# Rotary attention layer of a four-layer kernel: the rotation's work divided anew over ScalarE, GpSimd and VectorE

## The chip, the cores and the metric

The kernel runs on one core of one Trainium2 chip. The metric is the device time of one execution in microseconds, lower is better; each version is executed several times and the median counts.

## The reference

Four layers work on `x`, two batches of 256 tokens with 512 features. Each layer adds a gated attention and then a gated feed-forward part. The attentions differ; the second one (L1) rotates its queries and keys:

```
def _rope(x):                       # x: (B, H, S, 128)
    ...
    cos = concatenate([cos(ang), cos(ang)], axis=-1)
    sin = concatenate([sin(ang), sin(ang)], axis=-1)
    x1, x2 = (x[..., :64], x[..., 64:])
    rot = concatenate([-x2, x1], axis=-1)
    return x * cos + rot * sin

queries = _rope((q @ Wq.T) per head)    # 32 heads of 128
keys    = _rope((k @ Wk.T) per head)    # 8 key heads of 128, each for 4 query heads
scores  = queries . keys * 128 ** -0.5, causal (256 x 256, of 512 context rows only the first 256 count)
ctx     = softmax(scores) @ values
x       = x + tanh(g_xattn[1]) * (ctx @ Wd.T)
```

## The kernel before

One program, written engine by engine: each of the four attentions is a `Layer`, and `attn_sync`, `attn_tensor`, `attn_vector`, `attn_scalar` and `attn_gpsimd` write the queue of one engine each. Engines run their queues in order; they meet only through counted semaphores (`Counter`), one per kind of product: `q_mm` for a finished query projection, `q_f` for a rotated query before its sum, `q_sum` for the sum, `s_norm` for normalised probabilities, `wq_lo` for the low part of a piece of Wq, and so on.

All matrix products are done in three parts to keep precision: each operand is split in a high part (written by ScalarE's `activation`) and a low part (source less high part). The low parts of weights (`wq_lo`, `wkv_lo`, `wo_lo`) are GpSimd's, those of data (`q_lo`, `k_lo`, `v_lo`, `o_lo`, `pT_lo`) VectorE's. TensorE multiplies high by high, high by low and low by high.

The work goes by groups: a group is one key head with its four query heads. `walk` writes a prologue for group 0, then a hardware loop over pairs of groups, then the last two groups. A head has four slots, `j` = 0 to 3 (batch x half of the tokens), and the engines are shifted against each other: in slot `j` of a head the scores of two slots ahead are begun, and the probabilities of this slot are transposed and used. In the rotary layer:

- slot 1 of head h: TensorE projects the query of two heads ahead into the one bank `psQ`; it needs `wq_lo` and the bank free (`q_f`).
- the end of the same slot: VectorE rotates out of `psQ` into `qscr` (`q_front`, L739 to L741): feature d lies on partition d, so the exchange of halves is a product whose output lies 64 partitions away from its input. Three instructions: times cosine (128 partitions), upper and lower half times sine (64 each).
- slot 2: GpSimd first normalises the probabilities of slot 0 of the next head (L1041), then adds the two products (`q_sum`, L1058), and in heads 1 and 2 makes a low part of Wo (L1054).
- slot 3: ScalarE makes the query's high part (L949), which waits for `q_sum`. GpSimd normalises the next probabilities and makes a low part of Wq (L1048), for which the projection of the next head waits.
- slot 0 of the next head: VectorE makes the query's low part (L789).
- the next group's key is projected in slot 3 of head 1 and rotated in the same way (`use`, kind "k": VectorE into `scr`, sum on GpSimd L1066, high part on ScalarE L984, low part on VectorE L800); the values follow in head 2 (L839) and, transposed, in head 3 (ScalarE L996, VectorE L842).
- head 0, slots 1 to 3: TensorE's output projections of the group before (12 matmuls each), which wait for the output's low part (L794).

TensorE's matmuls are all written by a helper (L333), its transposes by L635. Cosines and sines lie in `mask_sb` behind the causal mask.

Of the kernel before, what the change touches and what calls it, by code (L numbers as in the profile page):

```python
# [24 lines left out]
ALU = mybir.AluOpType  # L25
ACT = mybir.ActivationFunctionType
AX = mybir.AxisListType

P = 128
B = 2  # L30
SQ = 256
# [45 lines left out]
            "av_mm o_hi o_lo x_mm x_act x_free k_f k_hi k_lo k_r k_diag").split()  # L77
# [44 lines left out]
class Layer:  # L122


    def __init__(self, index, sems):
# [18 lines left out]
        n = self.n  # L144
# [11 lines left out]
                     k_r=2 * n if self.rms else 0, k_diag=2 * n if self.rms else 0)  # L156
# [5 lines left out]
         self.x_free, self.k_f, self.k_hi, self.k_lo, self.k_r, self.k_diag) = counters  # L162
# [71 lines left out]
def program(nc, a, out, scratch):  # L234

    ctx = ExitStack()
    with ctx:
# [495 lines left out]
        def rotated(dve, src, dst):  # L733

            h = P // 2
            src = src.rearrange("p (b m) -> p b m", b=B)
            cos, sin = (trig[:, i, :].unsqueeze(1).broadcast_to([P, B, SQ]) for i in (0, 1))
            by_cos, by_sin = (dst[:, i, :].rearrange("p (b m) -> p b m", b=B) for i in (0, 1))
            dve.tensor_tensor(by_cos, src, cos, ALU.mult)  # L739
            dve.tensor_tensor(by_sin[0:h], src[h:P], sin[h:P], ALU.mult)  # L740
            return dve.tensor_tensor(by_sin[h:P], src[0:h], sin[0:h], ALU.mult)  # L741

        def attn_vector(dve, L):
# [32 lines left out]
            def q_front(g, h):  # L776
                L.q_mm.wait(dve, g.at(4, h + 1))
                L.q_f.inc(rotated(dve, psQ[:, :], qscr))
# [23 lines left out]
            def use(g, what, gp):  # L802
# [7 lines left out]
                if kind == "t" or (kind == "k" and not L.masked):  # L810
                    L.x_act.wait(dve, L.count(g, act_letters, what))
                elif kind == "k" and L.rms:
                    L.k_f.wait(dve, L.count(g, "k", what))
                else:
                    L.x_mm.wait(dve, k + 1)
# [9 lines left out]
                elif kind == "k" and L.rope:  # L825
                    ins = rotated(dve, X, scr)
# [89 lines left out]
        def attn_scalar(act, L):  # L916
# [27 lines left out]

            def q_high(g, h):
# [23 lines left out]
            def use(g, what, gp):  # L969
# [5 lines left out]
                if kind == "k" and L.rms:  # L975
                    L.x_mm.wait(act, k + 1)
                    L.k_f.inc(act.activation(ksq[:, i, :], X, ACT.Square))
                elif (kind == "k" and L.rope) or kind == "b":
# [20 lines left out]
            def prologue():  # L999
                for kind, piece in (("wq", 0), ("wkv", 0), ("wkv", 1), ("wq", 1)):  # L1000
                    w_high(kind, Group(0), piece)
                L.vec_dma.wait(act, L.n_vec)
                q_high(Group(0), 0)
                w_high("wq", Group(0), 2)
                for u in L.first:
                    use(None, u, Group(0))
                q_high(Group(0), 1)
                for j in range(L.ahead):
                    row_exp(Group(0), 0, j)

            def head(g, h):
                for j in range(4):
# [10 lines left out]
                    for u in L.slot_uses(g, h, j):  # L1023
                        if u[0] == "b" or (u[0] == "k" and L.rope):
                            late.append((g, u, g.to(1)))
                        elif u[0] not in ("out", "q"):
                            use(g, u, g.to(1))
# [4 lines left out]
                    if j == L.q_slot and L.step(g, h, 0, 8) and not L.rope:  # L1032
                        q_high(*L.step(g, h, 0, 8)[:2])
# [4 lines left out]
        def attn_gpsimd(pool, L):  # L1038
# [17 lines left out]
            def q_sum(g, h):  # L1056
                L.q_f.wait(pool, g.at(4, h + 1))
                L.q_sum.inc(pool.tensor_tensor(qscr[:, 0, :], qscr[:, 0, :], qscr[:, 1, :], ALU.add))  # L1058

            def use(g, what):  # L1060
# [553 lines left out]
```

How the kernel before makes its waits and increments, by code:

```python
    def wait(self, eng, value):  # L112
        if isinstance(value, int) and value <= 0:
            return
        eng.wait_ge(self.sem, value + self.base)
# [205 lines left out]
        def after(dve, ins):  # L322
            own[0] += 1
            ins.then_inc(dve_self, 1)
            dve.wait_ge(dve_self, own[0])
# [11 lines left out]
        def start_sync(sp):  # L338
            sp.dma_start(ident[:, :], a["c_ident"]).then_inc(const_dma, 16)
            sp.dma_start(ones[:, :], a["c_ones"]).then_inc(const_dma, 16)
            sp.dma_start(x_sb[:, :, :], a["x"].rearrange("b (t p) d -> p (b t) d", p=P)).then_inc(const_dma, 16)
            sp.dma_start(gates[:, 0:4], a["g_xattn"].partition_broadcast(P)).then_inc(gate_dma, 16)
            sp.dma_start(gates[:, 4:8], a["g_ffn"].partition_broadcast(P)).then_inc(gate_dma, 16)
            for c in range(DC):
                if c >= 2:
                    sp.wait_ge(ctx_lo, c - 1)
                sp.dma_start(p_sb[:, (c % 2) * 1024:(c % 2 + 1) * 1024],
                             a["ctxT"][:, c, :]).then_inc(ctx_dma[c % 2], 16)
# [1 line left out]
        def start_vector(dve):  # L350
            dve.memset(half[:, :], -0.5).then_inc(half_done, 1)
            for c in range(DC):
                dve.wait_ge(ctx_dma[c % 2], 16 * (c // 2 + 1))
                f = p_sb[:, (c % 2) * 1024:(c % 2 + 1) * 1024]
                dve.tensor_copy(cT_hi[:, c, :], f).then_inc(ctx_hi, 1)
                dve.wait_ge(ctx_hi, c + 1)
# [785 lines left out]
        def f0_tensor(pe):  # L1142
            pe.wait_ge(f0_w, 1)
            for t in range(NT):
```

## Time and profile before

| | |
|---|---|
| median of 3 executions | 2450.9 us (2448.56 to 2453.86) |
| the profiled execution | 2446.57 us, its span 2444.7 us |
| mean granted TensorE clock | 0.932 |
| busy in the span | PE 2058.0, DVE 1512.9, ACT 1034.7, POOL 1030.0 us |
| the rotary attention layer | about 715 to 1204 us |

PE is TensorE, PEld its weight loads, DVE VectorE, ACT ScalarE, POOL GpSimd, SP the engine that issues transfers. The span is the time from the first to the last instruction. A row with "idle before" gives how long the engine stood still just ahead of an instruction and which instruction of another engine ended that; "issue" means that the profile shows none. `L739` is line 739 of the kernel. The trace is of one execution, the median of others.

### The profile page before, as it was taken

To read this page: it belongs to the slowest core of one execution; us is meant where nothing else is said; L and a number is where in the kernel's file an instruction comes from. 1 tells how busy PE (TensorE), PEld (TensorE's weight loads), DVE (VectorE), ACT (ScalarE), POOL (GpSimd) and SP (SyncE) were. 2 spreads that over 40 slices of the span, in tenths; PEclk is the share of its full clock that TensorE was granted. 3 is DMA by queue.
4 is the path that set the end of the run, shared out by engine and by line. 5 is a ranking of instruction groups with operands and counts; after the bars stand their busy time and mean duration, and the time that the engine had idled before them with its cause. 6 is when DMAs were issued, how large, how long until landed. Compare 5 with 4: busy or idle time off the path is not lost.

```text
span 2444.7 us, 33604 instructions
## 1 busy us (share of the span) xinstructions
PE 2058.0 (84%) x10874; PEld 1700.0 (70%) x10874; DVE 1512.9 (62%) x2993; ACT 1034.7 (42%) x2320; POOL 1030.0 (42%) x955
## 2 busy tenths in 40 slices
PE   4898888988547878788888899997689999999986
PEld 3777777776435666666665788886567787787874
DVE  4777777777667666666533455554547766676664
ACT  2655565555314333333312344443135544455440
POOL 2555455554325444444332343333135544455540
PEclk9999999999868888888898999998789999999998
DMA  3212222121111111110021010000111100111001
GB/s 123 66 40 66 78 65 65 45 72 49 52 65 44 44 44 43 43 44 31 11 80 54 4 32 28 11 17 1 49 52 40 44 28 25 41 40 44 28 4 40
DMA packets 47042, 106.95 MB, mean 44 GB/s; under 512 B 6016, under 2 KB 21888, under 8 KB 43056
## 3 DMA queue, kind: packets, MB, share of 16 engines
q1 hardware_dynamic: 46896, 105.14, 13.6%
q8 instruction: 75, 1.23, 0.2%
q14 instruction: 71, 0.58, 0.1%
HBM read 98.37 MB, written 6.75 MB: 43 GB/s over the span
## 4 chain that ended last, share of the span: by engine, by line
PE 47%; issue 18%; DVE 14%; POOL 10%; ACT 7%; DMA 2%; SPq 0%; POOLq 0%; ACTq 0%; DVEq 0%
PE psX L333 18%; PE psS L333 7%; PE psQ L333 7%; PE psO L333 7%; POOL p_sb L1041 4%; PE psT L635 4%; DVE pT_lo L773 2%; ACT pT_hi L943 2%; POOL wo_lo L1054 2%; ACT dq_space L408 2%; POOL qscr L1058 1%; PE psT L333 1%; DVE nmax L763 1%; POOL wq_lo L1048 1%; ACT p_sb L936 1%
## 5 line engine op out<-in xcount | busy, mean ns | idle before, releaser
L1041 POOL TENSOR_TENSOR p_sb<-p_sb,rrec 128x512 f32<-128x512 f32 (+2 forms) x448 | 445.3, 994 | 950.5 <-DVE rrec L769 948.9
L943 ACT ACTIVATE pT_hi<-psT 128x512 fp32r<-128x512 f32 (+2 forms) x448 | 245.0, 547 | 413.7 <-PE psT L635 412.7
L773 DVE TENSOR_TENSOR pT_lo<-psT,pT_hi 128x512 fp32r<-128x512 f32 (+2 forms) x448 | 280.8, 627 | 113.2 <-ACT pT_hi L943 113.2
L333 PE MATMUL psO<-pT_hi,v_hi 128*128 128x256 f32 (+1 forms) x832 | 260.0, 313 | 61.4 <-DVE pT_lo L773 31.6
L635 PE MATMUL psT<-ident,p_sb 128*128 128x128 f32 x1600 | 262.0, 283 | 44.5 <-POOL p_sb L1041 44.3
L936 ACT ACTIVATE p_sb<-p_sb,nbias 128x512 f32<-128x512 f32 (+2 forms) x256 | 150.8, 589 | 270.9 <-DVE nbias L761 270.6
L635 PEld LDWEIGHTS psT<-ident,p_sb 128*128 128x128 f32 x1600 | 199.1, 144 | 94.1 <-POOL p_sb L1041 59.1
L333 PE MATMUL psX<-wo_hi,oT_hi 128*128 128x512 f32 (+1 forms) x448 | 187.0, 417 | 65.5 <-issue 65.5
L333 PE MATMUL psO<-pT_hi,v_lo 128*128 128x256 f32 (+1 forms) x832 | 239.7, 288 | 1.1 <-issue 1.1
L333 PE MATMUL psO<-pT_lo,v_hi 128*128 128x256 f32 (+1 forms) x832 | 240.1, 289 | 0.0
L333 PE MATMUL psQ<-xnT_hi,wq_hi 128*128 128x512 f32 (+1 forms) x448 | 198.8, 444 | 42.6 <-POOL wq_lo L1048 42.6
L333 PEld LDWEIGHTS psO<-pT_hi,v_hi 128*128 128x128 f32 (+1 forms) x832 | 157.5, 189 | 80.5 <-DVE pT_lo L773 65.4
L333 PE MATMUL psS<-kT_hi,q_hi 128*128 128x512 f32 (+2 forms) x448 | 178.9, 399 | 36.4 <-ACT p_sb L936 27.0
L936 ACT ACTIVATE p_sb<-psS,nbias 128x512 f32<-128x512 f32 (+1 forms) x192 | 145.3, 757 | 149.3 <-DVE nbias L765 149.3
L333 PE MATMUL psQ<-xnT_hi,wq_lo 128*128 128x512 f32 (+1 forms) x448 | 188.1, 420 | 0.0
L333 PE MATMUL psQ<-xnT_lo,wq_hi 128*128 128x512 f32 (+1 forms) x448 | 187.3, 418 | 0.0
L333 PE MATMUL psX<-wo_hi,oT_lo 128*128 128x512 f32 (+1 forms) x448 | 181.7, 406 | 0.0
L333 PE MATMUL psX<-wo_lo,oT_hi 128*128 128x512 f32 (+1 forms) x448 | 181.4, 405 | 0.0
L819 DVE SCALAR_TENSOR_TENSOR x_sb<-psX,gates,x_sb 128x512 f32<-128x512 f32 x112 | 83.9, 749 | 144.8 <-PE psX L333 144.8
L1048 POOL TENSOR_TENSOR wq_lo<-wq_f,wq_hi 128x512 fp32r<-128x512 f32 (+1 forms) x112 | 150.8, 1347 | 37.1 <-ACT wq_hi L925 37.1
L1054 POOL TENSOR_TENSOR wo_lo<-wo_f,wo_hi 128x512 fp32r<-128x512 f32 (+1 forms) x112 | 146.4, 1307 | 43.7 <-ACT wo_hi L931 43.1
L333 PE MATMUL psS<-kT_hi,q_lo 128*128 128x512 f32 (+2 forms) x448 | 164.7, 368 | 0.0
(313 smaller groups left out, 4845.8 us busy)
## 6 DMA issues: line engine op xcount, KB each, us to landing
wq_f<-in_a_wq SPq DMA_DIRECT2D x96, 256.0 KB, 2.6
wo_f<-in_a_wo SPq DMA_DIRECT2D x24, 1024.0 KB, 7.3
wkv_f<-in_a_wkv SPq DMA_DIRECT2D x24, 512.0 KB, 4.1
mask_sb<-in_codes SPq DMA_DIRECT2D x32, 174.0 KB, 2.4
qscr<-in_amax SPq DMA_DIRECT2D x32, 174.0 KB, 2.3
w<-qscr SPq DMA_DIRECT2D x32, 174.0 KB, 1.9
wo_f<-in_f_wT SPq DMA_DIRECT2D x3, 1024.0 KB, 5.1
wq_f<-in_a_wq SPq DMA_DIRECT2D x16, 192.0 KB, 2.4
```

Of the source, the lines that this page charges most:

```text
L333: mm = pe.matmul(dst, w, m, start=(first and k == 0), stop=(last and k == n - 1))
L408: ins = act.activation(tiles[q], dq_codes[h % 2], ACT.Copy, scale=slope, bias=NF4[c] - slope * c)
L635: mm = pe.transpose(t_view(L, j)[:, m, :], p_view(L, j)[:, m * P:(m + 1) * P], ident[:, :])
L763: L.s_nm.inc(dve.tensor_reduce(nmax[:, j:j + 1], s_view(L, j), AX.X, ALU.max, negate=True))
L773: L.t_lo.inc(dve.tensor_tensor(pT_view(L, pT_lo, j), t_view(L, j), pT_view(L, pT_hi, j).bitcast(F32), ALU.subtract))
L819: ins = dve.scalar_tensor_tensor(x_sb[:, i, :], X, gate, x_sb[:, i, :], ALU.mult, ALU.add)
L936: L.s_exp.inc(act.activation(p_view(L, j), src, ACT.Exp, bias=nbias[:, j:j + 1], scale=1.0 if L.masked else L.scale, accum_out=rsum[:, j:j ...
L943: L.t_hi.inc(act.activation(pT_view(L, pT_hi, j), t_view(L, j), ACT.Copy))
L1041: L.s_norm.inc(pool.tensor_tensor(p_view(L, j), p_view(L, j), rrec[:, j:j + 1].broadcast_to([P, L.open(j)]), ALU.mult))
L1048: L.wq_lo.inc(pool.tensor_tensor(lo, f, hi.bitcast(F32), ALU.subtract))
L1054: L.wo_lo.inc(pool.tensor_tensor(lo, f, hi.bitcast(F32), ALU.subtract))
L1058: L.q_sum.inc(pool.tensor_tensor(qscr[:, 0, :], qscr[:, 0, :], qscr[:, 1, :], ALU.add))
```

## The change

The rotation is divided over three engines. ScalarE copies the projection out of PSUM with its halves exchanged (`swapped`, two 64-partition copies) into the second half of `qscr` or `scr`. VectorE waits for these copies and makes the cosine product alone (`by_cos`). GpSimd multiplies the exchanged copy by the sines in place (`by_sin`), waits for its own result, and adds. The host's table of sines changes its signs to suit. Four counters are added (`q_swap`, `k_swap`, `q_sin`, `k_sin`). ScalarE's swap of a query is put at the end of slot 1; that of a key into slot 3 of head 1, behind the query's high part.

```diff
-        def rotated(dve, src, dst):
+        def swapped(act, src, dst):
 
             h = P // 2
-            src = src.rearrange("p (b m) -> p b m", b=B)
-            cos, sin = (trig[:, i, :].unsqueeze(1).broadcast_to([P, B, SQ]) for i in (0, 1))
-            by_cos, by_sin = (dst[:, i, :].rearrange("p (b m) -> p b m", b=B) for i in (0, 1))
-            dve.tensor_tensor(by_cos, src, cos, ALU.mult)
-            dve.tensor_tensor(by_sin[0:h], src[h:P], sin[h:P], ALU.mult)
-            return dve.tensor_tensor(by_sin[h:P], src[0:h], sin[0:h], ALU.mult)
+            act.activation(dst[0:h], src[h:P], ACT.Copy)
+            return act.activation(dst[h:P], src[0:h], ACT.Copy)
+
+        def by_cos(dve, src, dst):
+
+            src, dst = (z.rearrange("p (b m) -> p b m", b=B) for z in (src, dst))
+            return dve.tensor_tensor(dst, src, trig[:, 0, :].unsqueeze(1).broadcast_to([P, B, SQ]), ALU.mult)
+
+        def by_sin(pool, dst):
+
+            dst = dst.rearrange("p (b m) -> p b m", b=B)
+            return pool.tensor_tensor(dst, dst, trig[:, 1, :].unsqueeze(1).broadcast_to([P, B, SQ]), ALU.mult)
...
             def q_front(g, h):
-                L.q_mm.wait(dve, g.at(4, h + 1))
-                L.q_f.inc(rotated(dve, psQ[:, :], qscr))
+                L.q_swap.wait(dve, g.at(4, h + 1))
+                L.q_f.inc(by_cos(dve, psQ[:, :], qscr[:, 0, :]))
...
+                elif kind == "k" and L.rope:
+                    L.k_swap.wait(dve, L.count(g, "k", what))
...
-                    ins = rotated(dve, X, scr)
+                    ins = by_cos(dve, X, scr[:, 0, :])
                     late.append((g, i, kpar))
...
+            def q_swap(g, h):
+                L.q_mm.wait(act, g.at(4, h + 1))
+                L.q_swap.inc(swapped(act, psQ[:, :], qscr[:, 1, :]))
...
+                elif what[0] == "k" and L.rope and swap:
+                    L.x_mm.wait(act, k + 1)
+                    L.k_swap.inc(swapped(act, X, scr[:, 1, :]))
...
                     for u in L.slot_uses(g, h, j):
+                        if u[0] == "k" and L.rope:
+                            use(g, u, g.to(1), swap=True)
...
-                    if j == L.q_slot and L.step(g, h, 0, 8) and not L.rope:
-                        q_high(*L.step(g, h, 0, 8)[:2])
+                    if j == L.q_slot and L.step(g, h, 0, 8):
+                        (q_swap if L.rope else q_high)(*L.step(g, h, 0, 8)[:2])
...
             def q_sum(g, h):
                 L.q_f.wait(pool, g.at(4, h + 1))
+                L.q_sin.inc(by_sin(pool, qscr[:, 1, :]))
+                L.q_sin.wait(pool, g.at(4, h + 1))
                 L.q_sum.inc(pool.tensor_tensor(qscr[:, 0, :], qscr[:, 0, :], qscr[:, 1, :], ALU.add))
...
                     L.x_free.wait(pool, k + 1)
+                    L.k_sin.inc(by_sin(pool, scr[:, 1, :]))
+                    L.k_sin.wait(pool, L.count(g, "k", what))
                     L.k_f.inc(pool.tensor_tensor(scr[:, 0, :], scr[:, 0, :], scr[:, 1, :], ALU.add))
```

## Rows read from the trace of the kernel before

**Rows 1.** Busy time by engine, the rotary layer. Columns: stretch, us, then PE, PEld, DVE, ACT, POOL.
```profile
715.00:1204.00 489.00, 391.24 (x1894) 324.12 (x1893) 311.36 (x750) 185.87 (x540) 224.84 (x244) 0.87 0.12 41
```

**Rows 2.** Waits of the rotary layer: who waited for whom, us in total, times, longest.
```profile
DVE qscr L739 <- PE psQ L333: 46.1, 24, 2.9
...
PE psQ L333 <- POOL wq_lo L1048: 27.8, 15, 3.6
...
PE psT L635 <- POOL p_sb L1041: 24.0, 24, 2.1
```

**Rows 3.** Chain that ended last, in order of time: start, us, what.
```profile
896.73 1.29 POOL qscr L1058
```

**Rows 4.** Groups of instructions by line and form, 745 to 1112 us.
```profile
L1058 POOL TENSOR_TENSOR qscr<-qscr 128x512 f32<-128x512 f32 x25 | 32.2, 1286 | 0.0
...
L740 DVE TENSOR_TENSOR qscr<-psQ,mask_sb 64x512 f32<-64x512 f32 x24 | 16.6, 693 | 0.3
L739 DVE TENSOR_TENSOR qscr<-psQ,mask_sb 128x512 f32<-128x512 f32 x24 | 16.5, 689 | 35.4 <-PE psQ L333 35.4
```

**Rows 5.** Groups of GpSimd by form, whole span.
```profile
L1041 POOL TENSOR_TENSOR p_sb<-p_sb,rrec 128x512 f32<-128x512 f32 x256 | 274.0, 1071 | 508.7 <-DVE rrec L769 507.9
```

**Rows 6.** Timeline, head 2 of one group, GpSimd and TensorE: start, us, what.
```profile
896.73 1.30 POOL L1058 TENSOR_TENSOR qscr<-qscr 128x512 f32<-128x512 f32 x1
897.98 1.29 POOL L1054 TENSOR_TENSOR wo_lo<-wo_f,wo_hi 128x512 fp32r<-128x512 f32 x1
...
899.89 0.44 PE L635 MATMUL psT<-ident,p_sb 128*128 128x128 f32 x2 [1.06 <-POOL p_sb L1041]
901.19 0.49 PE L333 MATMUL psQ<-xnT_hi,wq_hi 128*128 128x512 f32 x1 [0.86 <-POOL wq_lo L1048]
```

**Rows 7.** Timeline, head 3 into head 0, ScalarE and TensorE.
```profile
911.02 0.63 ACT L949 ACTIVATE q_hi<-qscr 128x512 fp32r<-128x512 f32 x1 [0.29 <-POOL qscr L1058]
911.56 0.58 ACT L996 ACTIVATE v_hi<-psX 128x512 fp32r<-128x512 f32 x1
...
915.40 0.76 PE L333 MATMUL psX<-wo_hi,oT_hi 128*128 128x512 f32 x1 [3.28 <-issue]
```

**Rows 8.** Timeline, the key's rotation in two groups (883 and 942 us).
```profile
883.06 0.69 DVE L739 TENSOR_TENSOR scr<-psX,mask_sb 128x512 f32<-128x512 f32 x1 [0.97 <-PE psX L333]
...
942.61 0.63 ACT L949 ACTIVATE q_hi<-qscr 128x512 fp32r<-128x512 f32 x1 [0.31 <-POOL qscr L1058]
...
944.61 1.26 POOL L1066 TENSOR_TENSOR scr<-scr 128x512 f32<-128x512 f32 x1 [0.21 <-DVE scr L741]
...
945.83 1.78 POOL L1048 TENSOR_TENSOR wq_lo<-wq_f,wq_hi 128x512 fp32r<-128x512 f32 x1
...
946.73 1.43 DVE L800 TENSOR_TENSOR kT_lo<-scr,kT_hi 128x512 fp32r<-128x512 f32 x1 [0.25 <-ACT kT_hi L984]
...
947.74 0.79 PE L333 MATMUL psQ<-xnT_hi,wq_hi 128*128 128x512 f32 x1 [2.85 <-POOL wq_lo L1048]
```

**Rows 9.** Timeline of GpSimd, head 0 into head 1.
```profile
934.76 0.77 POOL L1041 TENSOR_TENSOR p_sb<-p_sb,rrec 128x128 f32<-128x128 f32 x1 [3.54 <-DVE rrec L769]
```

**Rows 10.** Timeline of GpSimd, first layer: a result and the instruction that waits for it.
```profile
74.53 0.93 POOL L435 TENSOR_TENSOR qscr<-dq_space,qscr 128x348 f32<-128x348 f32 x1 [0.52 <-DVE qscr L430]
75.60 0.93 POOL L438 TENSOR_TENSOR qscr<-qscr 128x348 f32<-128x348 f32 x1
```

**Rows 11.** Windows of two query projections; the granted clock is the third number from the end.
```profile
948.00:953.00 5.00, 5.00 (x13) 3.90 (x14) 1.99 (x6) 0.60 (x2) 2.28 (x3) 0.52 0.17 52
961.00:965.00 4.00, 3.49 (x18) 2.98 (x19) 3.19 (x7) 0.67 (x3) 1.80 (x3) 1.00 0.60 187
```

**Rows 12.** Timeline of TensorE and VectorE at these projections.
```profile
953.14 0.69 DVE L739 TENSOR_TENSOR qscr<-psQ,mask_sb 128x512 f32<-128x512 f32 x1 [2.78 <-PE psQ L333]
...
961.51 0.49 PE L333 MATMUL psQ<-xnT_hi,wq_hi 128*128 128x512 f32 x1 [0.86 <-POOL wq_lo L1048]
...
964.57 0.69 DVE L739 TENSOR_TENSOR qscr<-psQ,mask_sb 128x512 f32<-128x512 f32 x1 [0.44 <-PE psQ L333]
```

More of the change, by code:

```diff
@@ L76 @@
             "q_mm q_hi q_lo q_f q_sum q_r s_mm s_nm s_mask s_max s_exp s_rec s_norm t_mm t_hi t_lo "
-            "av_mm o_hi o_lo x_mm x_act x_free k_f k_hi k_lo k_r k_diag").split()
+            "av_mm o_hi o_lo x_mm x_act x_free k_f k_hi k_lo k_r k_diag q_swap k_swap q_sin k_sin").split()
 class Group:
@@ L155, in __init__ @@
                      q_sum=4 * n if self.rope else 0, q_r=4 * n if self.rms else 0,
-                     k_r=2 * n if self.rms else 0, k_diag=2 * n if self.rms else 0)
+                     k_r=2 * n if self.rms else 0, k_diag=2 * n if self.rms else 0,
+                     q_swap=4 * n if self.rope else 0, k_swap=n if self.rope else 0,
+                     q_sin=4 * n if self.rope else 0, k_sin=n if self.rope else 0)
         counters = [Counter(sems[name][0], sems[name][1]) for name in COUNTERS]
@@ L161, in __init__ @@
          self.t_mm, self.t_hi, self.t_lo, self.av_mm, self.o_hi, self.o_lo, self.x_mm, self.x_act,
-         self.x_free, self.k_f, self.k_hi, self.k_lo, self.k_r, self.k_diag) = counters
+         self.x_free, self.k_f, self.k_hi, self.k_lo, self.k_r, self.k_diag, self.q_swap, self.k_swap,
+         self.q_sin, self.k_sin) = counters
         self.wq_dma = (wqA_dma, wqB_dma)
@@ L967, in o_high, with use @@
                 L.o_hi.inc(act.activation(oT_hi[0:hd, h, :], psO[0:hd, :], ACT.Copy))
-            def use(g, what, gp):
+            def use(g, what, gp, swap=False):
                 k, bank = L.use(g, what)
@@ L1002, in prologue @@
                 L.vec_dma.wait(act, L.n_vec)
+                if L.rope:
+                    q_swap(Group(0), 0)
                 q_high(Group(0), 0)
@@ L1005, in prologue @@
                 for u in L.first:
+                    if u[0] == "k" and L.rope:
+                        use(None, u, Group(0), swap=True)
                     use(None, u, Group(0))
+                if L.rope:
+                    q_swap(Group(0), 1)
                 q_high(Group(0), 1)
@@ L1023, in head @@
                     for u in L.slot_uses(g, h, j):
+                        if u[0] == "k" and L.rope:
+                            use(g, u, g.to(1), swap=True)
                         if u[0] == "b" or (u[0] == "k" and L.rope):
@@ L1553 @@
     cos, sin = np.cos(ang).T, np.sin(ang).T
-    cos, sin = np.concatenate([cos, cos]), np.concatenate([sin, -sin])
+    cos, sin = np.concatenate([cos, cos]), np.concatenate([-sin, sin])
     causal = np.where(np.arange(SQ)[:, None] >= np.arange(SQ)[None, :], 0.0, NEG).astype(np.float32)
```

## The prediction

> **What bounds the kernel now.** I read the stretches first. The rotation exists only in the second of the four attention layers, which lies between about 715 and 1204 us of the span [rows 1]. There TensorE is busy 391 of 489 us, VectorE 311 (64%), GpSimd 225 (46%), ScalarE 186. So 98 us of TensorE's time are gaps, and what the change is worth is what it does to these gaps. All other layers run unchanged code.
>
> Then the waits of that stretch [rows 2]: TensorE waits 27.8 us for the low part of Wq, which GpSimd makes, and 24.0 us for the normalised probabilities, which GpSimd makes too. VectorE, before the first product of a query rotation, waits 46.1 us for TensorE's query projection, in 24 of 32 heads. So VectorE, though the busier engine, is mostly early at the rotation; GpSimd, though idle half of the time, is late where TensorE needs it.
>
> The chain in order of time says which instruction: GpSimd's query sum stands on it, three times in each group of four heads in the middle of the layer; one of them is shown [rows 3].
>
> Last the timeline of single heads. After the query sum of head 2 GpSimd runs without a pause: sum 896.73, low part of Wo 897.98, then norm, then low part of Wq; TensorE waits 1.06 us for that norm and 0.86 us for that Wq [rows 6]. In head 3 the sum ends near 911.0, ScalarE's query copy starts at 911.02, its value copy at 911.56 stands behind it, and through VectorE's queue (value low part, row maxima, output low part) TensorE's output projection starts at 915.40 after 3.28 us of gap [rows 7]. In head 1 the key's rotation follows: ScalarE's query copy at 942.61, GpSimd's key sum 944.61, low part of Wq 945.83 to 947.61, TensorE at 947.74 after 2.85 us [rows 8]. In head 0 GpSimd stands idle 3.54 us after its queue [rows 9] while TensorE runs output projections.
>
> **The change, part by part.** Removed from VectorE: two 64-partition products of 0.69 us per rotation [rows 4], 40 rotations (32 query heads, 8 keys), 55 us of busy time. VectorE keeps one, 0.69.
>
> Added to ScalarE: two 64-partition copies out of PSUM. The trace has none; the nearest is the 128-partition copy of 0.58 us, the next instruction on ScalarE starting 0.54 us after the one before [rows 7]. That half the partitions don't halve the time is seen in VectorE's products, 693 ns for 64 and 689 for 128 [rows 4]. So the swap takes 0.54 + 0.58 = 1.1 us. Bounds: 0.6 (if half the partitions did halve it) and 1.3. Behind it on ScalarE stands the probability copy of slot 2, whose input comes only after the query projection, and whose reader on VectorE has the cosine product and row maxima ahead of it; that covers it. Without that cover it is 1.1 us per head.
>
> VectorE now waits for the swap: its part ends 1.1 + 0.69 = 1.8 us after the projection, where it was 3 x 0.69 = 2.1. Gain 0.3 us where VectorE was early, which is most heads.
>
> Added to GpSimd: one 128x512 product with two inputs. The nearest row is the query sum itself, same size, same inputs, 1286 ns [rows 4]; the lower bound is the normalisation with one broadcast column, 1071 ns [rows 5]. The sum then waits for the engine's own result. Such a pair is in the first layer: starts at 74.53 and 75.60 for an instruction of 0.93, so 0.14 us between them [rows 10]; the lower bound is nothing. I take 1.29 + 0.14 = 1.43 us. The query sum thus ends 1.43 - 0.3 = 1.13 us later.
>
> Heads 2 and 3: norm and low part of Wq stand right behind it, and in head 3 the query copy does, so TensorE's gap grows by 1.13 us in each [rows 6, 7]. Head 0: the 3.54 us of idle GpSimd behind it [rows 9] swallow it; nothing. If that cover were gone it would cost 1.13 more.
>
> Head 1, the key. ScalarE's query copy waits for the query sum and starts as that ends, at 942.61 now [rows 8]; 1.13 later is just over 943.7. And the key's swap stands behind that copy in ScalarE's queue: copy to 944.2, swap to 945.35, cosine product to 946.05, sine product with its wait to 947.5, key sum to 948.75. It ended at 945.87 [rows 8]: 2.9 us later. Low part of Wq and TensorE's projection follow at once. In the other group of the loop's pair the key's projection came out of TensorE later (VectorE waited 0.97 us for it at 883.06 [rows 8]), so the query copy is hidden in that wait and 0.8 of the 2.9 falls away: 2.1. Mean 2.5.
>
> Sum. Seven groups rotate a next key: 7 x (2.5 + 1.13 + 1.13) = 33.3. Prologue: three rotations in series before TensorE's first transposes: 3 x 1.1, less 0.5 because the first swap lies beside two memsets: 2.8. Head 0 of the first group has no output projections to hide under, and head 1 of the last group still rotates: 2 x 1.1. Total 38 us. The profiled execution took 2446.57 us (span 2444.7), so it would take 2485; the median of the runs is 4.3 us above it, so I say 2450.9 + 38 = 2489 us.
>
> TensorE's clock is the term left out. After the gap in head 1 the projection at 948 ran at a granted clock of 0.52, the 1.2 GHz level; the one at 961 ran at 1.00, 2.4 GHz, though a gap of 0.86 us lay before it [rows 11]. By the start of TensorE's projection and of VectorE's first product behind it, the one took 3.1 us (961.51 to 964.57), the other 5.4 (947.74 to 953.14) [rows 8, 12]. If the longer gap takes its clock too, 2.3 us more in each of four pairs of groups, 9 us. The Trainium skill, "Perfetto Trace Analysis", Matmul Optimizations, says that the engine scales with utilisation and that matmuls should run back to back; the trace agrees, 0.52 after the gap.
>
> A rule speaks against the change. The rows show 0.69 us on VectorE against 1.29 on GpSimd for a product of one size [rows 4]. The Trainium skill, "GPSIMD Engine Reference", Engine selection, gives elementwise products to VectorE, as GpSimd is about twice as slow with two inputs; the trace agrees, 1.9 times. By its factor of 2 the sum would be about 3 us more.
>
> **Rivals.** (a) VectorE's relief decides: faster. It is the busiest helper [rows 1]. In 8 query rotations and 6 or so keys it was not waiting for TensorE and sheds up to 1.4 us each, 20 us; the others give 24 x 0.3 = 7. If GpSimd's idle half took its product whole, the time is 2424. It decides if GpSimd stands idle just ahead of the norm and Wq for which TensorE waits; [rows 6, 8] show it at work there. The Trainium skill, "Perfetto Trace Analysis", Identifying the Most-Contended Engine, would have the busiest engine relieved first, which is this case; [rows 2] speak against it here. Chance 0.07.
> (b) It is all hidden: GpSimd's product fits into its idle time and VectorE's 0.3 us is worth nothing either, 2451. Against it: the same rows. Chance 0.06.
> (c) Only a part arrives: the key's queue behind the query copy costs no more than 1.13, the product is 1.07 us, the self wait nothing: 38 - 7 x 1.4 - 29 x 0.33 = 19 us (29 products on the path: four in each of seven groups and one more), 2470. Chance 0.13.
> (d) Worse: GpSimd's product meets VectorE instructions with both inputs in SBUF. The key's low part took 1.43 us where it overlapped GpSimd [rows 8], VectorE's other instructions of that size 0.69 [rows 4]. If each of the 21 heads on the path loses another 0.7 us, 15 us, and the clock its 9: 2513. The product runs right after the cosine product, where VectorE works on scores out of PSUM, so it should mostly miss them. The Trainium skill, "SBUF — State Buffer", Who interferes with whom, says that a VectorE instruction with two SBUF inputs and a GpSimd one that reads SBUF shut each other out; the trace agrees, 1.43 against 0.69. Chance 0.10.
>
> **How the numbers follow.** The forecast, 2475 to 2506, has 0.64; (c) lies between 2456 and 2475. Slower by over 0.2% (5 us, about what a measurement of this kernel can tell): 0.64 + 0.13 + 0.10 = 0.87. The range takes in the low bounds (2470, and 2 for the spread of the runs) and the clock with some collisions (38 + 9 + 8 = 55): 2468 to 2506.
>
> **What the new profile would show.** The cosine product at 0.69 and alone; two ScalarE copies of about 0.58; GpSimd's products at about 1.29, 40 of them; GpSimd's busy time in the layer up by 52 us, VectorE's down by 55. The layer, 489 us, becomes 527. TensorE's waits for Wq and for the norm grow by about 7 x 3.6 us together. Wrong if GpSimd shows idle time ahead of its norm in heads 2 and 3, if the key's swap does not queue behind the query copy, or if the sine product is near 1.0 us.

## The result, and the profile after

| | before | changed |
|---|---|---|
| median of the runs, us | 2451.8 (2448.6 to 2453.9) | 2490.2 (2483.6 to 2494.9) |
| profiled execution, us | 2446.6, span 2444.7 | 2485.8, span 2484.0 |
| mean granted TensorE clock | 0.932 | 0.918 |

The changed kernel is slower: ratio 1.0156, 95% interval 1.0124 to 1.0188, which is 38 us; 2489 was forecast. Over the whole kernel VectorE's busy time fell from 1512.9 to 1455.5 us, GpSimd's rose from 1030.0 to 1079.7, ScalarE's from 1034.7 to 1084.4.

I measure the rotary layer between two landmarks that both traces have: the first matmul of its first query projection and the first of its last output projection. Before, that is 710.15 to 1203.25 us, 493.1; after, 715.38 to 1246.12, 530.7. The layer is 37.6 us longer. Windows of the changed kernel, over this layer and over the two projections that follow GpSimd's late work in one group (columns as in [rows 1]; the clock is the third number from the end):

```profile
715.38:1246.12 530.74, 398.14 (x1904) 328.29 (x1905) 252.14 (x670) 235.59 (x621) 277.76 (x287) 0.83 0.12 39
...
910.40:915.00 4.60, 4.58 (x14) 3.69 (x15) 2.31 (x6) 0.74 (x4) 2.55 (x3) 0.64 0.17 57
924.40:928.50 4.10, 4.10 (x12) 3.31 (x13) 2.24 (x6) 0.60 (x2) 1.27 (x2) 0.64 0.74 224
```

The same window of before, for the comparison:

```profile
710.15:1203.25 493.10, 395.34 (x1905) 327.34 (x1905) 311.36 (x750) 185.94 (x541) 228.40 (x247) 0.86 0.13 42
```

TensorE's busy time grew by 2.8 us only; the other 34.8 us are gaps. VectorE lost 59 us of work there, and GpSimd and ScalarE gained 49 and 50. The waits of the changed kernel's layer say whose gaps they are (engine, waited for, us in total, times, longest):

```profile
ACT qscr L739 <- PE psQ L336: 98.8, 31, 6.9
...
DVE qscr L745 <- ACT qscr L740: 85.7, 32, 5.0
...
PE psT L638 <- POOL p_sb L1067: 51.5, 33, 3.6
...
PE psQ L336 <- POOL wq_lo L1074: 43.0, 16, 4.7
```

TensorE's wait for the normalised probabilities rose from 24.0 us [rows 2] to 51.5. Its wait for Wq's low part is 43.0 against 31.5 before over the same landmarks ([rows 2] begin a little later and so leave one of 3.6 us out). Together that is 39.0 us more, and it is GpSimd that TensorE waits for both times; what makes GpSimd late for Wq is another matter (e3 and e1 below). The new instructions of the query rotation, by line and form (duration in ns as least/median/most):

```profile
L739 ACT ACTIVATE qscr<-psQ x32: 593/594/596, 720.7 to 1221.4; 64x512 f32<-64x512 f32 x32
L740 ACT ACTIVATE qscr<-psQ x32: 588/591/592, 721.3 to 1222.0; 64x512 f32<-64x512 f32 x32
L745 DVE TENSOR_TENSOR qscr<-psQ,mask_sb x32: 691/692/695, 722.0 to 1222.6; 128x512 f32<-128x512 f32 x32
L750 POOL TENSOR_TENSOR qscr<-qscr,mask_sb x32: 1271/1290/1304, 722.7 to 1225.0; 128x512 f32<-128x512 f32 x32
```

The timeline of one group of the changed kernel: head 1 with the key (903 to 911 us), head 2 (918 to 925), head 3 (932 to 940). It answers to [rows 6, 7, 8].

```profile
903.48 0.63 ACT L964 ACTIVATE q_hi<-qscr 128x512 fp32r<-128x512 f32 x1 [1.68 <-POOL qscr L1086]
904.14 0.59 ACT L739 ACTIVATE scr<-psX 64x512 f32<-64x512 f32 x1
904.74 0.59 ACT L740 ACTIVATE scr<-psX 64x512 f32<-64x512 f32 x1
...
905.36 0.69 DVE L745 TENSOR_TENSOR scr<-psX,mask_sb 128x512 f32<-128x512 f32 x1 [3.36 <-ACT scr L740]
...
906.13 1.26 POOL L750 TENSOR_TENSOR scr<-scr,mask_sb 128x512 f32<-128x512 f32 x1 [0.89 <-DVE scr L745]
907.47 1.59 POOL L1096 TENSOR_TENSOR scr<-scr 128x512 f32<-128x512 f32 x1
909.02 1.26 POOL L1074 TENSOR_TENSOR wq_lo<-wq_f,wq_hi 128x512 fp32r<-128x512 f32 x1
...
910.42 0.79 PE L336 MATMUL psQ<-xnT_hi,wq_hi 128*128 128x512 f32 x1 [4.68 <-POOL wq_lo L1074]
...
918.58 1.28 POOL L750 TENSOR_TENSOR qscr<-qscr,mask_sb 128x512 f32<-128x512 f32 x1
919.94 1.29 POOL L1086 TENSOR_TENSOR qscr<-qscr 128x512 f32<-128x512 f32 x1
921.19 1.27 POOL L1080 TENSOR_TENSOR wo_lo<-wo_f,wo_hi 128x512 fp32r<-128x512 f32 x1
922.42 0.61 POOL L1067 TENSOR_TENSOR p_sb<-p_sb,rrec 128x256 f32<-128x256 f32 x1
...
923.09 0.44 PE L638 MATMUL psT<-ident,p_sb 128*128 128x128 f32 x2 [2.12 <-POOL p_sb L1067]
924.38 0.79 PE L336 MATMUL psQ<-xnT_hi,wq_hi 128*128 128x512 f32 x1 [0.86 <-POOL wq_lo L1074]
...
935.65 0.69 PE L638 MATMUL psT<-ident,p_sb 128*128 128x128 f32 x2 [0.96 <-POOL p_sb L1067]
...
939.47 0.77 PE L336 MATMUL psX<-wo_hi,oT_hi 128*128 128x512 f32 x1 [3.13 <-issue]
```

The reader should follow GpSimd's column from 918.58: product, sum, low part of Wo and norm without a pause, and TensorE starts as the norm ends, after 2.12 us of gap where [rows 6] have 1.06. Then 903.48: the key's swap stands behind the query copy, and VectorE, GpSimd and TensorE start one after the other behind it.

One thing is in the trace of before and missing after. At the turn of the layer's loop (behind head 0 of groups 2 and 4) VectorE stood still with nothing that it waited for ("issue"). Timeline of before:

```profile
869.85 0.75 DVE L819 SCALAR_TENSOR_TENSOR x_sb<-psX,gates,x_sb 128x512 f32<-128x512 f32 x1 [1.97 <-PE psX L333]
872.86 0.29 DVE L757 SCALAR_TENSOR_TENSOR p_sb<-psS,mask_sb 128x128 f32<-128x128 f32 x1 [2.26 <-issue]
```

The period of a group (start of one head 0's output projection to the next) shows both effects. The table gives differences in us; for the prediction its terms are 2.8 + 1.1 + 4.8 in the first row and 4.8 (mean) for each group that rotates a next key.

| group | before | after | difference | predicted |
|---|---|---|---|---|
| layer start to first output projection | 82.6 | 94.0 | +11.4 | 8.7 |
| 1, 3, 5 | 58.6, 58.8, 58.7 | 65.2, 64.9, 64.8 | +6.6, +6.1, +6.1 | 4.8 each |
| 2, 4 (with the turn of the loop) | 64.1, 64.1 | 64.9, 64.9 | +0.8, +0.8 | 4.8 each |
| 6 | 60.5 | 64.8 | +4.2 | 4.8 |
| last, no next key | 45.7 | 47.3 | +1.6 | 1.1 |
| sum | | | +37.6 | 38 |

### The profile page after: what moved, and what is told of

Read it like the earlier page. It is cut to its first block, busy times and chain, and to the rows that moved or that the text cites. A ratio compares the mean times of both kernels' runs of the same rounds, so it can differ in the third digit from the quotient of the medians.

```text
span 2484.0 us, 33695 instructions
## 1 busy us (share of the span) xinstructions
PE 2071.7 (83%) x10874; PEld 1710.7 (69%) x10874; DVE 1455.5 (59%) x2913; ACT 1084.4 (44%) x2400; POOL 1079.7 (43%) x995
## 4 chain that ended last, share of the span: by engine, by line
PE 47%; issue 18%; DVE 13%; POOL 12%; ACT 7%; DMA 2%; SPq 0%; POOLq 0%; ACTq 0%; DVEq 0%
PE psX L336 18%; PE psS L336 7%; PE psQ L336 7%; PE psO L336 7%; POOL p_sb L1067 4%; PE psT L638 4%; DVE pT_lo L782 2%; POOL wo_lo L1080 2%; ACT pT_hi L954 2%; ACT dq_space L411 1%; POOL qscr L750 1%; POOL wq_lo L1074 1%; PE psT L336 1%; DVE nmax L772 1%; ACT p_sb L947 1%
## 5 line engine op out<-in xcount | busy, mean ns | idle before, releaser
L336 PE MATMUL psX<-wo_hi,oT_hi 128*128 128x512 f32 (+1 forms) x448 | 190.6, 425 | 64.9 <-issue 64.9
L336 PE MATMUL psS<-kT_lo,q_hi 128*128 128x512 f32 (+2 forms) x448 | 165.7, 370 | 0.0
```

What stands on the lines that cost most here:

```text
L336: mm = pe.matmul(dst, w, m, start=(first and k == 0), stop=(last and k == n - 1))
```

## The experiments

Of each run, "layer" is the time between the two landmarks (493.1 before, 530.7 changed), and the ratio is to the kernel before, with its 95% interval. The ratio of each is taken against executions of the kernel before made beside it; their medians were 2451.1 us (e1, e2, e4, e9), 2451.9 (e3, e5, ea, eb) and 2454.6 (f1 to f4), so of these runs ratios compare better than medians.

The layer's time comes from one execution of each kernel. The rest of the kernel is the same code in all, and took 1951 to 1966 us in these executions, so a layer and a median can differ in what they say by some us. How far the layer's own time varies between executions isn't shown, as each kernel has one trace.

| run | median, us | ratio | layer, us |
|---|---|---|---|
| before | 2451.8 | 1 | 493.1 |
| changed | 2490.2 | 1.0156 (1.0124 to 1.0188) | 530.7 |
| e1, key's swap ahead of the query copy | 2490.1 | 1.0150 (1.0127 to 1.0173) | 526.9 |
| e2, sine product on VectorE | 2466.3 | 1.0064 (1.0042 to 1.0086) | 506.7 |
| e3, before with a GpSimd product | 2492.9 | 1.0158 (1.0134 to 1.0182) | 533.8 |
| e4, changed without sine product | 2440.2 | 0.9948 (0.9928 to 0.9969) | 475.3 |
| e5, before, query sum later | 2446.7 | 0.9971 (0.9957 to 0.9986) | 487.8 |
| e9, before without VectorE's sine products | 2387.7 | 0.9731 (0.9704 to 0.9757) | 432.0 |
| ea, e5 and query rotation behind the scores | 2463.9 | 1.0048 (1.0034 to 1.0063) | 504.0 |
| eb, ea and the key's rotation as well | 2442.1 | 0.9960 (0.9947 to 0.9974) | 485.5 |
| f1, changed with two tiny writes a rotation | 2497.3 | 1.0170 (1.0149 to 1.0191) | 537.4 |
| f2, e5 with the low part first | 2462.7 | 1.0037 (1.0020 to 1.0054) | 503.7 |
| f3, eb with the low part first | 2450.2 | 0.9994 (0.9977 to 1.0011) | 486.4 |
| f4, changed, swap and sums late | 2491.2 | 1.0145 (1.0115 to 1.0175) | 527.1 |

The theory is that GpSimd's added product, standing in its queue ahead of the norm and of Wq's low part, makes the whole loss. The rivals: the swap on ScalarE makes it; or the order of the key's swap does; or the relief of VectorE would decide if it came alone.

**e3, the suspected cost alone.** GpSimd makes one more product ahead of the query sum of the kernel before, into a tile that nothing reads:

```
                 L.q_f.wait(pool, g.at(4, h + 1))
+                pool.tensor_tensor(kx_lo[:, 0, :], qscr[:, 0, :], qscr[:, 1, :], ALU.mult)
```

> The kernel before with one more 128x512 product on GpSimd ahead of each query sum, written to a tile that this layer does not use; VectorE and ScalarE unchanged. It is the change's cost on GpSimd by itself, without the key's. Queue theory: 1.25 us later at heads 1, 2 and 3 of seven groups, 26 us, 2.5 in the prologue and 2.5 at the ends: about 2482 us. Rival, GpSimd's idle half takes it: 2451 us.

2492.9 us, 11 more than expected, and no different in total from the changed kernel. Its window and its waits in the layer:

```profile
713.01:1246.80 533.79, 408.50 (x1905) 335.81 (x1905) 317.18 (x750) 187.11 (x541) 266.75 (x279) 0.83 0.12 39
...
PE psT L635 <- POOL p_sb L1041: 51.9, 33, 3.4
PE psQ L333 <- POOL wq_lo L1048: 28.4, 16, 3.9
```

TensorE's wait for the norm is that of the changed kernel (51.5). So the product alone, in the 32 query rotations and with no swap and no key product, costs as much as the change: 40.7 us in the layer. The change's other parts (swap, key product, relief of VectorE) must then come to near nothing together, if the parts add up.

The two losses aren't made of the same pieces, though. In e3 27.5 of the 40.7 us are gaps (125.3 against 97.8), as much as the wait for the norm has grown, and 13.2 are longer busy time of TensorE for the same matmuls; in the changed kernel it is 34.8 and 2.8. And the wait for Wq's low part, 31.5 us before and 43.0 in the changed kernel, is 28.4 here. So the queries' product delays the norm; the growth at Wq comes only with the key's steps.

**e2 and e4, the change without GpSimd's product.** In e2 VectorE takes it, in e4 nobody:

```
-                L.q_f.inc(by_cos(dve, psQ[:, :], qscr[:, 0, :]))
+                by_cos(dve, psQ[:, :], qscr[:, 0, :])
+                L.q_f.inc(by_sin(dve, qscr[:, 1, :]))      (these three lines e2 only)
...
-                L.q_sin.inc(by_sin(pool, qscr[:, 1, :]))
-                L.q_sin.wait(pool, g.at(4, h + 1))         (e2 and e4)
```

The key's rotation is edited in the same way. e4 leaves the multiplication by the sines out.

> The changed kernel with the sine product on VectorE, behind its cosine product; GpSimd only adds, ScalarE swaps as before. Theory, a serial chain of swap, VectorE, GpSimd, in which each microsecond counts wherever it stands: a product costs 0.65 us on VectorE and 1.36 us on GpSimd, so 0.7 us less at each of three query rotations of a group, and 1.4 for the key with the copy ahead of it; 2.8 x 7 and 2 for the ends: about 2468 us. Rival, the waits that the swap adds are the cause and not GpSimd's product: 2490 us or more.

> The changed kernel without any sine product (the rotation leaves out the multiplication by the sines; the rest, swap and sum too, is kept). Theory: GpSimd's product and its wait are 1.36 us of the 1.18 us net at each query rotation, so that without it the swap alone is left, which VectorE's shorter part pays back: 1.36 us less at heads 2 and 3, 2.7 us less at head 1, 38 us over seven groups, 3 for the ends: about 2449 us, as the kernel before. Rival, half of the loss is the swap and the order of ScalarE's queue: 2470 us.

e2 was met within 2 us (2466.3). e4 came out at 2440.2, 9 below its expectation. Waits of e4:

```profile
PE psQ L336 <- POOL wq_lo L1074: 34.6, 16, 3.8
...
PE psT L638 <- POOL p_sb L1067: 21.5, 26, 2.3
```

Without its products on GpSimd (queries' and keys') the changed kernel is faster than before by 17.8 us in the layer; by the ratio it is 13 us in the whole kernel (8 to 18). The products cost 55.4 us in the layer (530.7 less 475.3), and 50.0 between the medians. e3, without the keys' product, had 40.7; the keys' product alone was not run. The window of e4's layer splits them:

```profile
718.63:1193.91 475.28, 383.35 (x1905) 318.45 (x1905) 255.13 (x670) 234.13 (x621) 228.74 (x247) 0.89 0.13 43
```

TensorE is busy 383.4 us for the same 1905 matmuls, 398.1 in the changed kernel: 14.8 us are the clock (0.89 against 0.83). The gaps are 91.9 against 132.6 us, so the products add 40.7 us of gaps; the prediction's 29 products on the path at 1.36 us (its 1.29 and the self wait) are 39.4. The 17.8 us that the rest gives back are accounted for below.

**e9, the relief alone.** The kernel before without its two sine products on VectorE (it leaves the rotated half out and adds zeros instead, which two writes in the prologue make):

```
-            dve.tensor_tensor(by_cos, src, cos, ALU.mult)
-            dve.tensor_tensor(by_sin[0:h], src[h:P], sin[h:P], ALU.mult)
-            return dve.tensor_tensor(by_sin[h:P], src[0:h], sin[0:h], ALU.mult)
+            return dve.tensor_tensor(by_cos, src, cos, ALU.mult)
```

> The kernel before without its two sine products on VectorE (the rotation leaves out the rotated half; a half of zeros is added on GpSimd as before, after two memsets in the prologue). It measures VectorE's relief by itself, with no swap and no work for GpSimd. Serial-chain theory: VectorE's part ends 1.4 us earlier and everything behind it moves up, at heads 1, 2 and 3 of seven groups: 1.4 x 3 x 7 = 29, 4 in the prologue, 2 at the ends: about 2416 us. Rival, VectorE is early at the rotation and its relief is worth next to nothing: 2446 to 2452 us.

2387.7, where 2416 was expected: the relief is worth 61 us in the layer. Its window there:

```profile
720.35:1152.35 432.00, 369.23 (x1904) 311.22 (x1905) 248.98 (x672) 189.00 (x541) 228.52 (x247) 0.92 0.15 48
```

The gaps are 62.8 us, 97.8 before: 35 less; TensorE's busy time is 26 less, at a clock of 0.92. Behind a projection VectorE's part ends 0.7 us after it and no longer 2.1, and TensorE's wait for the norm nearly vanishes:

```profile
PE psT L635 <- POOL p_sb L1041: 5.8, 6, 2.3
```

So rival (a) had more in it than it was given: VectorE's part lies on the path of most heads. But it lies there as a latency behind the projection, and the change gives back only 0.18 us of it, as the swap stands in the same place. The 61 us are not that latency alone: VectorE's stand at the turn of the loop is missing here too, and groups 2 and 4 gained 10 to 11 us where groups 1, 3 and 5 gained 5 to 6.

**e1, the key's swap moved.** In the changed kernel ScalarE exchanges the key's halves ahead of the query copy.

```
+                    for u in L.slot_uses(g, h, j):
+                        if u[0] == "k" and L.rope:
+                            use(g, u, g.to(1), swap=True)
                     if j == 3 and L.rope and L.step(g, h, 0, 8):
                         q_high(*L.step(g, h, 0, 8)[:2])
                     while late:
                         use(*late.pop(0))
                     for u in L.slot_uses(g, h, j):
-                        if u[0] == "k" and L.rope:
-                            use(g, u, g.to(1), swap=True)
```

> The changed kernel with one difference: in slot 3 of head 1 ScalarE makes the key's swap ahead of the query copy instead of behind it. Queue theory: in the changed kernel's trace the key's projection ends at 901.93, the query copy starts only at 903.48 and the swap ends at 905.35. With the swap first the cosine product can end near 903.9, but GpSimd is busy with its queue until 905.24, where its sine product of the key started at 906.13: 0.9 us less in each of seven groups, 6 us, about 2484 us. Rival, the order on ScalarE does not matter because GpSimd sets the key's path: 2490 us.

The median didn't move (2490.1); the layer is 3.9 us shorter, which is within the spread of the total. TensorE's wait for Wq's low part fell from 43.0 to 36.4 us, the 6 us that the queue theory names, so more than half of the growth at Wq is the swap's place behind the query copy. Timeline of e1:

```profile
911.13 0.79 PE L336 MATMUL psQ<-xnT_hi,wq_hi 128*128 128x512 f32 x1 [3.75 <-POOL wq_lo L1075]
...
925.59 0.71 PE L336 MATMUL psQ<-xnT_hi,wq_hi 128*128 128x512 f32 x1 [0.86 <-POOL wq_lo L1075]
```

The gap is 3.75 us and not 4.68, as the queue predicts. Most of that is lost again: from its first matmul to its last the projection behind it takes 5.01 us, 4.52 in the changed kernel, and that of head 2 4.60 against 4.39. In e1 the gap in the key's head is shorter and the matmuls behind it run slower; why the clock falls just there is not shown.

**f1, the stand of VectorE at the turn of the loop.** It is in the layer of before, e2, e3, e5, ea, eb, f2 and f3, where VectorE has two or three instructions a rotation, and not in that of the changed kernel, e1, e4, e9 and f4, where it has one. f1 adds two in idle time:

```
             def q_front(g, h):
+                dve.memset(tiny[:, 0:2], 0.0)
+                dve.memset(tiny[:, 2:4], 0.0)
                 L.q_swap.wait(dve, g.at(4, h + 1))
```

(and the same ahead of the key's wait).

> The changed kernel with two VectorE writes of 128x2 elements ahead of VectorE's wait in every rotation, so that a rotation has three VectorE instructions again, as before the change; they lie in the time in which VectorE waits for the projection. Theory: VectorE's stand of 2.26 us without a releaser at the turn of the loop, which is in the trace of before and not in that of the change, comes with the number of VectorE's instructions in the loop's body, and comes back: 2 turns by 2 to 2.5 us, 2494 to 2496 us in all, and in the trace 'issue' of over 2 us on VectorE, once in each turn of the loop. Rival: it came from where the waits fell (ScalarE or TensorE late at that place), or it lies in a gap that has room for it now: no stand of over 1 us and 2490 us.

2497.3 us, and the layer 6.6 us longer than that of the changed kernel. In the whole kernel the difference isn't shown: the ratio is 1.0170, the changed kernel's 1.0156, and the intervals overlap. The trace decides here. Its timeline, and the same place in the changed kernel (behind the last output projection of group 1, where the loop turns):

```profile
895.03 0.75 DVE L835 SCALAR_TENSOR_TENSOR x_sb<-psX,gates,x_sb 128x512 f32<-128x512 f32 x1 [1.97 <-PE psX L337]
898.78 0.29 DVE L767 SCALAR_TENSOR_TENSOR p_sb<-psS,mask_sb 128x128 f32<-128x128 f32 x1 [3.00 <-issue]
```

```profile
892.66 0.75 DVE L830 SCALAR_TENSOR_TENSOR x_sb<-psX,gates,x_sb 128x512 f32<-128x512 f32 x1 [1.97 <-PE psX L336]
893.33 0.28 DVE L766 SCALAR_TENSOR_TENSOR p_sb<-psS,mask_sb 128x128 f32<-128x128 f32 x1
```

The stand is back at both turns (3.00 and 2.56 us). The period of the group at the first turn is 69.6 us against 64.9, at the second 66.4 against 64.9. So the stand comes with VectorE's added instructions, though they take 0.06 us each, in time in which VectorE waits anyway. Whether it is their number or something that goes with it, and what happens in the stand (the trace names nothing), stays open.

**e5, ea, eb, f2, f3: can the sum wait?** If GpSimd's place ahead of the norm costs this much, the sum of the kernel before might stand behind it. e5:

```
-                    if j == 2 and L.rope and L.step(g, h, 0, 8):
-                        q_sum(*L.step(g, h, 0, 8)[:2])
...
+                    if j == 3 and L.rope and L.step(g, h, 0, 8):
+                        q_sum(*L.step(g, h, 0, 8)[:2])
```

with the query's high and low part a slot later on ScalarE and VectorE. ea also lets VectorE rotate the query behind the scores of slot 2; eb defers the key's rotation too.

> The kernel before with the query sum taken out of GpSimd's way: it is made at the end of slot 3, behind the norm and the low part of Wq, and the query's high and low parts are made a slot later. No instruction is added. Queue theory: the 1.25 us of the sum leave the path at heads 2 and 3 (in head 1 the key's sum ends last): 2 x 1.25 x 7 = 17, about 2433 us, and less if TensorE's clock gains as it did without the sine products on VectorE. Rival, GpSimd's order does not matter and only what VectorE does right behind the projection counts: 2451 us.

> As the run with the later sum, and VectorE rotates a query at the end of slot 2 instead of the end of slot 1, so behind the row maxima of the scores that TensorE finished meanwhile. Latency theory, the time from the projection to the next norm is what TensorE waits for: VectorE's 2.1 us leave the path at three heads of a group, more than the 1.4 us whose removal gave 63 us, and GpSimd's 1.25 at two: about 2385 us. Rival, VectorE's load is the bound, not its order: no better than the run with the later sum, about 2433 us.

> As the run before, and the key's rotation is put off as well: VectorE makes it behind slot 0 of head 2, GpSimd's key sum follows in slot 1 behind the low part of Wo, high and low parts in slot 2. Latency theory: head 1's path loses the key's product and sum, which set TensorE's wait for Wq there (2.85 us in the trace of before): 2 to 3 us in each of seven groups, about 2367 us. Rival, the key's path is hidden once the queries' is short: 2385 us.

e5 and eb are faster than before by 0.3 and 0.4%, ea is slower, and all miss what was expected. Waits of eb:

```profile
PE psS L333 <- DVE q_lo L790: 41.8, 22, 4.4
PE psO L333 <- DVE pT_lo L773: 25.3, 13, 2.4
PE psQ L333 <- POOL wq_lo L1056: 13.1, 13, 3.6
```

GpSimd is in time now (13.1 us for Wq, 2.9 for the norm), and TensorE waits 41.8 us for the query's low part instead. f2 and f3 move that part to the head of VectorE's slot 1:

```
+                    if j == 1 and L.rope and L.step(g, h, 0, 4):
+                        q_low(*L.step(g, h, 0, 4)[:2])
                     if j == 1 and h == 0 and (g.off or g.loop is not None):
```

> The kernel before with the query's sum late in slot 3 (as in the run with the sum later), and the query's low part as the first work of VectorE in slot 1 instead of behind row maximum, transposed probabilities and reciprocal. In the run with the sum later TensorE waited 31.0 us for that low part ahead of the scores (20 times over 0.5 us), against 27.8 and 24.0 us for Wq's low part and the normalisation before. Theory (the low part was only walked too late): of the 31 us some 25 go, 2422 us. Rival: VectorE then waits at the head of slot 1 for ScalarE's high part, and the row maximum behind it, and so the chain of the next slot, comes later by as much: 2447 us, no better than the run with the sum later.

> The kernel before with both rotations and their sums behind the scores' chain (2442.1 us), and the query's low part as VectorE's first work of slot 1. There TensorE waited 41.8 us for the low part (22 times), and only 13.1 us for Wq's low part and nothing to speak of for the normalisation. Theory (the low part was walked too late): some 30 of the 41.8 us go, 2412 us. Rival (the query's rotation is then simply too late, whatever the order of VectorE's work, as the high part that ScalarE makes comes late too): 2440 us, and the wait for the low part stays over 30 us.

Both rivals won: f2 is 16 us slower than e5, f3 8 slower than eb. (The traces of f3 and eb show less, layers of 486.4 and 485.5 us; f3's is of its fastest execution.) Waits of f3:

```profile
PE psX L333 <- issue: 30.7, 8, 4.3
PE psO L333 <- DVE oT_lo L795: 29.3, 23, 2.0
PE psO L333 <- DVE pT_lo L773: 28.2, 17, 2.4
...
PE psS L333 <- DVE q_lo L790: 5.2, 3, 1.9
```

The wait for the low part has gone (5.2 us), and the time stands elsewhere: 29.3 us before the weighted values for the output's low part, which VectorE now makes later (1.5 in eb), and 30.7 before the output projection (12.1 in eb). So the loop behaves like a ring in which the projection, the rotation, the scores and the norm follow each other; a step taken out of one wait turned up in the next in each of these placements. eb is the version that beats both kernels, by 10 us over the one before.

**f4, the changed kernel with its instructions placed otherwise.** VectorE's cosine product first, the swap behind the exponential of slot 2, product and sum at the end of slot 3:

```
-                L.q_swap.wait(dve, g.at(4, h + 1))
...
+                L.q_mm.wait(dve, g.at(4, h + 1))
...
-                L.q_mm.wait(act, g.at(4, h + 1))
+                L.q_f.wait(act, g.at(4, h + 1))
```

> The changed kernel, with the same three instructions placed otherwise: the vector engine's cosine product first (it no longer waits for the exchange), the exchange behind ScalarE's exponential of slot 2, GpSimd's sine product and sum at the end of slot 3 behind the normalisation and Wq's low part, the key's sum likewise, and the low part first in VectorE's slot 1. If GpSimd's product costs only by standing ahead of the normalisation and of Wq's low part, most of the 39 us by which those two waits grew goes, and what is left is 5 to 15 us more of waits for a late high and low part: 2455 to 2465 us. Rival: GpSimd is then as late for the next slot's normalisation, as its work of slot 3 has grown by 1.4 us, and the query's parts are late on top: 2485 us or more.

2491.2: the rival. Waits of f4:

```profile
PE psX L336 <- issue: 38.0, 7, 5.4
PE psO L336 <- DVE oT_lo L804: 30.9, 24, 1.6
PE psS L336 <- DVE q_lo L799: 28.5, 9, 3.6
PE psQ L336 <- POOL wq_lo L1077: 15.1, 9, 3.8
...
PE psT L638 <- POOL p_sb L1070: 6.3, 4, 4.9
```

The waits for the norm and Wq have shrunk from 94.5 to 21.4 us, and the total hasn't moved; other waits took their place (38.0, 30.9 and 28.5). That the chain of four engines is longer wherever it stands is the likely reading, and isn't tested further. An overlap of the swap with the cosine product, both reading one PSUM bank, was not tried.

**One period for different waits.** The windows of group 3 in the changed kernel, in e1 and in f4 (columns as in [rows 1]):

```profile
939.47:1004.32 64.85, 49.98 (x244) 41.28 (x245) 31.77 (x85) 29.73 (x78) 35.00 (x37) 0.84 0.12 40
...
940.90:1005.73 64.83, 50.48 (x245) 41.73 (x245) 32.85 (x85) 29.51 (x78) 34.98 (x37) 0.87 0.12 40
...
939.89:1004.82 64.93, 49.43 (x245) 41.28 (x245) 30.48 (x85) 29.54 (x78) 33.25 (x37) 0.87 0.12 40
```

The gaps are 14.9, 14.4 and 15.5 us, the periods 64.8 to 64.9; the busy time of TensorE makes up for the gaps. From group 2 to group 6 all three kernels keep to 64.7 to 64.9 us, and e3 does in its groups 3, 5 and 6, with gaps of 13.5 us in group 3. What holds the period there no run shows. It means that the equal totals of e1, e3 and f4 are weaker evidence than they look: in these kernels a shorter wait isn't seen in the period. That GpSimd's products are the cause rests on e4 and e2, whose periods do change (58.0, and 61.5 to 64.2), and on the wait for the norm.

## Why the prediction was right

**The total** was 38 us, and the layer grew by 37.6; the medians are 38.3 apart.

**The swap** was put at 1.1 us. Its two copies take 0.59 each, so half the partitions save nothing, and their starts are 0.60 apart, not 0.54: 1.2 us. VectorE's part ends 1.96 us after the projection (1.27 to its start, 0.69), so the gain is 0.18 and not 0.3.

**GpSimd's product** is 1.29 as predicted. The self wait is smaller: 918.58 + 1.28 to 919.94 leaves 0.08 us, where 0.14 was taken. The query sum ends 1.36 - 0.18 = 1.18 later; 1.13 was said.

**Head 2**: the gap grew from 1.06 to 2.12 us, by 1.06. **Head 3**: the gap before the output projection hardly moved (3.28 in one group, now 3.13), and a new one of 0.96 stands before a transpose; 0.8 us in this group, 1.4 in the other of the pair. The size was right, the place half wrong: the norm took the wait. **Head 0**: nothing, as said.

**Head 1**: the key's swap does queue behind the query copy. TensorE's wait for Wq is 4.68 us against 3.59 and 2.85, and 1.83 stands in front of it at a transpose, where before one of the groups has 1.00 and the other none: 2.9 and 2.7 us more, mean 2.8, and 2.5 was said. e1 shows the swap's share: with the swap first the gap is 0.93 us shorter. The pair's difference was 0.2, not the 0.8 reasoned. The key sum took 1.59 us instead of 1.26 [rows 8], as it now meets VectorE's query low part; that is rival (d)'s mechanism, at a third of a microsecond in one head of four.

**The clock** was left out. In a group without the turn of the loop TensorE's gaps grew by 2.7 + 1.0 + 1.4 = 5.1 us, which is the prediction's 5.2 (2.9 + 1.13 + 1.13), but the group by 6.1. The projection of head 2 takes 4.4 us where [rows 12] have 3.1, at a granted clock of 0.64 where [rows 11] have 1.00: 1.3 us, not the 2.3 of the upper bound, and only in groups without the turn of the loop (in the others it took 4.6 us before). And 0.9 comes back in head 1, whose projection takes 4.5 us, before 5.4, at 0.64 against 0.52. The rest, 0.6 us, lies in small pieces that I didn't follow. Over the layer TensorE's busy time grew by 2.8 us; the upper bound had 9. The Trainium skill, "Perfetto Trace Analysis", Matmul Optimizations, says that the matmul engine scales power with utilisation, so that matmuls should run back to back in batches. Four layers agree with it: 98 us of gaps at 0.86, 133 at 0.83, and in e4 and e9 92 at 0.89 and 63 at 0.92. Two don't fall in line: f3 has 116 us of gaps at 0.91 and TensorE busy for 370 us, e3 125 at 0.83 and 408.5. So the sum of the gaps doesn't price the clock here; e3's 13.2 us and f3's 25 less are more than the whole term was worth in the change.

**What was missed** is the turn of the loop. Groups 2 and 4 grew by 0.8 us where 4.8 was said, since what the turn of the loop cost before (VectorE's stand of 2.3 us and what goes with it) is gone with the two instructions: against the groups beside them that is 5.4 us less, twice, 11 us. How much of the 11 is the stand's own is not shown; f1, which brings it back, adds 4.7 and 1.6 us to these groups. These two groups came out 8 us under the prediction, and the rest of the layer 7 over it. The total was right because two errors cancel, which is luck. The waits say the same: TensorE's for Wq and for the norm were to grow by 25 us (7 x 3.6) and grew by 39.0.

**The rivals.** (a), VectorE's relief, is refuted as a forecast, not as a mechanism: e9 shows 61 us of it. The change bought 32 x 0.18 = 6 us and the 11 of the turn, together 17; e4, which has both and no product, measured 17.8 in its trace. The Trainium skill, "Perfetto Trace Analysis", Identifying the Most-Contended Engine, would have the most occupied engine optimised first, TensorE included, judged by its weight loads. In this layer these take 324 us and VectorE 311 [rows 1], so the rule doesn't point at VectorE alone. e9 agrees that relieving VectorE pays (0.973), and the change shows that the relief is void when the new steps stand on the same path. (b) fell with e3 and e4, and (c) with the rows above: the product is 1.29 us and not 1.07, and head 1 pays 2.8. (d) fell in its size: GpSimd's products stayed at 1271 to 1304 ns, and VectorE's 32 low parts of the queries took 30.7 us in all, 30.5 before.

## What to carry to other kernels

Price a moved instruction by where it stands between two waits of the bounding engine, not by its engine's load: here, in the layers' traces, 59 us off VectorE bought 18, and 49 us onto GpSimd cost 55. Ask of each added step which late product stands behind it in the same queue; placing it elsewhere in a ring of dependent steps moved the wait and did not save the time (f2, f3, f4). Gaps that are added or removed can bring a part of their size again in TensorE's busy time (e4: 15 us on 41, e3: 13 on 27), but the sum of gaps doesn't say how much (f3: 25 us less at 18 more of gaps than before). And compare periods of like iterations: a total can be right by two errors, and kernels with different waits can share one period.

## What the runs showed of the hardware

- VectorE stands still for 2.2 to 3.0 us at the turn of the layer's loop with no releaser in the trace when it has two or three instructions a rotation (before, e2, e3, e5, ea, eb, f1 to f3), and not with one (changed, e1, e4, e9, f4). Two writes of 128x2 elements a rotation bring it back (f1), and the layer of that trace is 6.6 us longer.
- A ScalarE copy out of PSUM of 64 partitions takes 0.59 us, one of 128 takes 0.58 [rows 7]; two in a row start 0.60 apart, so they don't overlap.
- A GpSimd instruction that needs the result of the one before it starts 0.07 to 0.08 us after its end (0.14 in [rows 10]).
- A shorter gap needn't be a gain: e1's is 0.93 us shorter, and TensorE's two projections behind it take 0.7 us more; the period of the group stays at 64.8 us.
